# Attention shares of a graph network read from two PSUM banks in turn by the multiplication with the values

## The reference

```
q, k, v = x@qw+qb, x@kw+kb, x@vw+vb          # (N, 8 heads, 16)
alpha = sum(q[dst] * k[src], -1) * SCALE
a = exp(alpha - segment_max(alpha, dst)[dst])
a = a / segment_sum(a, dst)[dst]
out = segment_sum(v[src] * a[:, :, None], dst).reshape(N, 128) + x@sw + sb
```

## Time and profile before

| what | value |
|---|---|
| median of 3 runs | 7398.97 us (7388.78 to 7423.69) |
| the profiled execution | 7369.88 us, span 7368.1 us |
| edge stages of the two convolutions | about 160 to 1565 us and 1700 to 3075 us of the span |
| busy over the span | PE 47%, DVE 55%, ACT 21%, POOL 57% |
| granted TensorE clock over the span | 0.64 |

### The profile page before, as it was taken

How to read it: one execution, slowest core, us unless ns; L and a number is a source line. 1 busy time by engine, 2 the same in 40 slices (tenths; PEclk the granted TensorE clock), 3 DMA queues, 4 the chain that set the end, 5 groups by cost and what they waited for, 6 DMA issues and landing times. The chain is left out here.

```text
span 7368.1 us, 52378 instructions
## 1 busy us (share of the span) xinstructions
PE 3449.0 (47%) x13922; PEld 2171.5 (29%) x13922; DVE 4050.4 (55%) x5309; ACT 1566.7 (21%) x3305; POOL 4165.2 (57%) x4238
## 2 busy tenths in 40 slices
PE   4556565664566565684233334323333422333456
PEld 3445444453455444542011111111111101111223
DVE  5556666664666666675344444434555344445498
ACT  1111111111111111102222222222222222222223
POOL 2556555635565656435766664766665676667321
PEclk7666666675666666786556656555565655556577
DMA  3455555534555555374223232322322222323242
GB/s 100 133 154 159 149 156 155 158 96 138 152 166 152 160 154 157 93 276 109 86 88 93 93 95 70 97 81 91 97 94 88 81 87 83 93 92 98 98 152 89
DMA packets 542429, 877.90 MB, mean 119 GB/s; under 512 B 85288, under 2 KB 383761, under 8 KB 534092
## 3 DMA queue, kind: packets, MB, share of 16 engines
q0 software_dynamic: 167776, 479.21, 21.8%
q1 hardware_dynamic: 374376, 395.35, 17.1%
HBM read 553.75 MB, written 320.47 MB: 119 GB/s over the span
## 5 line engine op out<-in xcount | busy, mean ns | idle before, releaser
L1330 POOL DMA_INDIRECT big<-h_tab,big x2352 | 2245.3, 955 | 1147.8 <-issue 824.1
L598 POOL DMA_INDIRECT big<-kv_tab,big x1664 | 1625.5, 977 | 1185.6 <-DVE big L808 663.4
L1376 PE MATMUL psum<-big 128*128 128x512 f32 x1176 | 1057.8, 1052 | 2255.7 <-ACT big L1353 1292.5
L1413 DVE TENSOR_TENSOR psum<-psum,big 128x1024 f32<-128x1024 f32 x294 | 556.1, 1892 | 1761.4 <-remote 1278.6
L1376 PEld LDWEIGHTS psum<-big 128*128 128x128 f32 x1176 | 333.0, 313 | 2818.8 <-ACT big L1353 1427.8
L1347 ACT COPY big<-big 128x1024 f32<-128x1024 f32 x294 | 567.4, 1930 | 2514.8 <-DVE big L1396 2030.9
L725 PE MATMUL psum<-big 128*128 128x128 bf16 x1408 | 568.7, 404 | 952.4 <-ACT big L679 479.1
L769 PE MATMUL psum<-big 128*128 128x136 f32 x3328 | 777.4, 392 | 184.9 <-DVE big L839 81.4
L679 ACT COPY big<-psum 125x128 f32<-125x128 f32 x1408 | 376.5, 267 | 2042.6 <-PE psum L725 818.0
L769 PEld LDWEIGHTS psum<-big 128*128 128x128 f32 x3328 | 668.7, 281 | 247.1 <-issue 205.3
L803 DVE TENSOR_TENSOR big<-psum,big 128x512 f32<-128x512 f32 x416 | 286.7, 689 | 804.1 <-remote 632.7
(11 more groups left out here) (392 smaller groups left out, 3376.1 us busy)
## 6 DMA issues: line engine op xcount, KB each, us to landing
run_tab<-big SPq DMA_DIRECT2D x294, 512.0 KB
snap_tab<-big SPq DMA_DIRECT2D x176, 448.0 KB
item_tab<-big SPq DMA_DIRECT2D x208, 272.0 KB
big<-loc_tab SPq DMA_DIRECT2D x104, 512.0 KB
big<-h_tab,big POOLq DMA_INDIRECT x2352
big<-kv_tab,big POOLq DMA_INDIRECT x1664
snap_tab<-big SPq DMA_DIRECT2D x176, 52.0 KB
kv_tab<-big SPq DMA_DIRECT2D x12, 512.0 KB, 2.6
```

The lines of the kernel that those rows point to most:

```text
L598: nc.gpsimd.indirect_dma_start(out=kv_ring[:, b % SLOTS, k, :], out_offset=None, in_=kv_tab, in_offset=bass.IndirectOffsetOnAxis(ap=src_it ...
L1330: nc.gpsimd.indirect_dma_start(out=got[j % RING][:, k * D:(k + 1) * D], out_offset=None, in_=h_tab, in_offset=bass.IndirectOffsetOnAxis(ap ...
L1376: ins_ = nc.tensor.matmul(bank[2 * (j % DEEP) + k][:, :], ea_T[j % DEEP], w_blocks[:, k * 512:(k + 1) * 512], start=True, stop=True)
L1413: nc.vector.tensor_tensor(by_feature(msg[j % DEEP]), by_feature(msg[j % DEEP]), got[j % RING].rearrange("p (t f) -> p f t", f=D), ALU.add) ...
```

## The change

The transposes of the exponentials go alternately to bank 3 (even groups) and bank 6 (odd groups), and write their columns already in the order item, half, head: runs of 8 columns with a step of 16. ACT's copy into `share` stays, now without reordering, and L700 still reads `share`. The multiplication with the values reads the shares from the PSUM bank; it waits for `shared` as before. PE waits for the copy of the group before last in place of the last one, and in addition for `va_done` of the group before last, whose shares lay in the bank that it overwrites. No instruction changes its place.

```diff
+                turned_ex = [bank[3], bank[6]]
@@ ACT
                                 act.wait_ge(ex_T, g + 1)
                                 later(act, va_done, 8 * (g - 1))
-                                nc.scalar.copy(by_item(share[g % 2]), bank[3][:, 0:PAIR].rearrange("p (s i h) -> p s i h", s=2, h=HEADS)).then_inc(shared, 1)
+                                nc.scalar.copy(share[g % 2], turned_ex[g % 2][:, 0:PAIR]).then_inc(shared, 1)
@@ PE
                                 pe.wait_ge(ex_done, g + 1)
-                                later(pe, shared, g)
+                                later(pe, shared, g - 1)
+                                later(pe, va_done, 8 * (g - 1))
                                 for s in range(2):
-                                    ins_ = nc.tensor.transpose(bank[3][:, s * P:(s + 1) * P], ex[:, s * P:(s + 1) * P], ident[:, :])
+                                    ins_ = nc.tensor.transpose(by_item(turned_ex[g % 2][:, 0:PAIR])[:, s, :, :], ex[:, s * P:(s + 1) * P], ident[:, :])
                                 ins_.then_inc(ex_T, 1)
@@ DVE
                                 dve.wait_ge(shared, b // 8 + 1)
                                 later(dve, item_done, 2 * b - 2)
                                 nc.vector.tensor_tensor(va[b % 2][:, :, 0:D]..., kv[:, b % SLOTS, :, D:]...,
-                                                        share[b // 8 % 2][:, b % 8 * 32:(b % 8 + 1) * 32]....to_broadcast([P, 4, HEADS, CH]),
+                                                        turned_ex[b // 8 % 2][:, b % 8 * 32:(b % 8 + 1) * 32]....to_broadcast([P, 4, HEADS, CH]),
                                                         ALU.mult).then_inc(va_done, 1)
```

More of the change, by code:

```diff
@@ L808, in _ @@
                                 nc.vector.tensor_tensor(va[b % 2][:, :, 0:D].rearrange("p k (h c) -> p k h c", h=HEADS), kv[:, b % SLOTS, :, D:].rearrange("p k (h c) -> p k h c", h=HEADS),
-                                                        share[b // 8 % 2][:, b % 8 * 32:(b % 8 + 1) * 32].rearrange("p (k h) -> p k h", h=HEADS).unsqueeze(3).to_broadcast([P, 4, HEADS, CH]),
+                                                        turned_ex[b // 8 % 2][:, b % 8 * 32:(b % 8 + 1) * 32].rearrange("p (k h) -> p k h", h=HEADS).unsqueeze(3).to_broadcast([P, 4, HEADS, CH]),
                                                         ALU.mult).then_inc(va_done, 1)
```

## The result

The kernel with the change took 7440.25 us (median, 7420.12 to 7450.84) against 7396.96 us (7380.41 to 7423.69) for the kernel before on the same chip: 1.0054 [1.0038, 1.0070]. That is +43 us, where -4 was forecast, and it lies above the range. The profiled execution took 7450.84 us (span 7449.1), 81 us more than that of before. The execution of before lies 11 us under the fastest of the six timed ones (7380.41), and that of after is the slowest of its six, so this pair overstates the loss: the traces tell where it lies, and the medians how much it is.

What follows compares the result with a forecast made beforehand. No engine was full; POOL's gathers and DVE wait for each other in a ring with four batches between. DVE's +2.5 and POOL's -6.3 us gave about -4, other terms 0: 7399 to 7395 us, range 7356 to 7434.

Steps and rivals of the forecast that it cites:

- The waits: PE's looser wait for ACT's copy and its added wait at L741: all costed at 0.
- ACT's copy and the transposes: L687 without reordering, 394 ns against 387, and PE's stepped PSUM writes at 421 ns: both costed at 0.
- my straight line: ACT's dense copy of 256 columns, interpolated between 298 ns for 128 and 587 for 512: 394 ns.
- the bound of +20 us: Upper bound for PE's transposes, if stepped PSUM writes doubled their duration: at most about 20 us of the end.
- The multiplication, DVE's part: L808 with its second input in PSUM: 6 ns more for each of 416 instances, as L803, +2.5 us.
- Rivals B and C: L808 slower: B by PSUM reads of a repeated element, about 7475, chance 0.07; C by the skill's fixed term, 7440, 0.03.
- The multiplication, POOL's part: Gathers starting in L808 no longer stretched: POOL spared 12.7 us, half reaching the end, -6.3 us (bounds -12.7 and 0).
- The sum: Whole kernel: about -4 us, 7395 us; shifted meetings with other transfers taken as scatter of about 20 us either way.
- rival D: Edge stages: earlier gathers land ahead of other transfers and save long DVE waits, 42 us faster, about 7355, chance 0.10.
- The idle sums: POOL's idle time at L598 (663 us) and DVE's at L803 (633) should each stay within some 30 us.
- the 37: Refutation test: the forecast is wrong if the two edge stages together move by more than 37 us from 2780.

Runs made afterwards that it cites:

- few gathers: Three of four gathers left out from the 15th batch on: kernel before 0.8703 (6438.15 us), changed kernel 0.8695 (6432.38 us).
- The odd and even batches: Changed kernel with the shares read from SBUF again in even batches only, 1.0014, or in odd batches only, 1.0054, of the kernel before.
- five further comparisons: Without, with the change: rerun 1, 1.0038; slots back later 1.0092, 1.0106; fifteen slots 1.0008, 1.0039; one-hot ahead 0.9916, 0.9984; POOL memset 1.0013, 1.0108.
- a later release: POOL waits for the one-hot instead of the multiplication before reusing a slot: kernel before 1.0092, changed kernel 1.0106.
- the plain pair: The kernel before and the changed kernel with no other edit: 1.0054, and 1.0038 when run again.
- the one-hot first: DVE's one-hot moved ahead of the reduction, right behind the multiplication: kernel before 0.9916 (7284.7 us), changed kernel 0.9984 (7328.99 us).
- the memset in the changed kernel: Changed kernel with a one-column memset on POOL ahead of each batch's gathers: 1.0108 of the kernel before.

## Why the prediction was wrong

- **The waits: right as far as shown.** All of the change but the read is 0.9999, the added wait alone 1.0000. With the read there, the kernel that keeps the old wait too is at 1.0023, so that the looser wait has no share in the loss is not shown.
- **ACT's copy and the transposes: right.** No gain depends on the copy; it takes 374 ns instead of 387, better than the 394 of my straight line. PE writes runs of 8 with a step of 16 at 421 ns; the bound of +20 us was not needed.
- **The multiplication, DVE's part: right in substance, off in sign.** I put it at +6 ns, by L803; it is -6 ns (677 against 683), so -2.5 us rather than +2.5. With few gathers the changed kernel is no slower (6 us faster, within the intervals). Rivals B and C needed 89 and 65 ns more per instance: they fell.
- **The multiplication, POOL's part: the step that failed.** Its local half held: of 94 gathers that start in L810, none is stretched. I then took each one's excess as saved for POOL ("POOL is spared 12.7 us") and bounded what it is worth by -12.7 and 0. The first is false as the trace after has it: the next gather comes 0.2 us earlier and starts early enough in L818, 66 of 81 times with a hold-up, and the mean is 976 ns, not 969. The second is where the sign went wrong. I let a gather that isn't held up be at worst useless ("else they are lost in POOL's next wait"). The odd and even batches show that the read which removes these hold-ups in even turns costs 0.54%, and the one that keeps them there 0.14% or nothing.
- **The sum.** "An engine that shifts by a fraction of a microsecond also meets other transfers [...] I can't size that and treat it as scatter." It was no scatter but +43 us, and slower again in four of five further comparisons. The prediction's rival D had this mechanism but with a gain; its own words, that a shifted order "is as likely to be worse", should have been a second rival with a chance of its own.
- **The idle sums.** I wanted L598 and L803 to stay within 30 us. L803's counterpart has 6 us more in all, L598's wait for slots 75 more (663 to 738). The stages moved by 73 us in the traces, and the medians by 43, both beyond the 37 that I named as the refutation.

The Trainium skill, SBUF — State Buffer, section "Who interferes with whom", says that a VectorE instruction with two SBUF inputs contends with a GpSimd instruction that reads SBUF. The counts agree (96 of 99 against 0 of 94, and 257 of 271 in the one-hot); what it is worth to the kernel's time does not follow from it.

What stays open: how 0.13 us at a gather tips a turn of 6.7 us. I have the switch (the read in even turns) and its outcome, not the chain between them, nor why the loss is not seen with a later release, and may be smaller with the old wait. The pattern of waits goes with the loss in the plain pair, but not in the pair with the one-hot first, which still shows the gap.

## What to carry to other kernels

Where no engine is full and two of them wait for each other by turns, contention that is removed is not time gained: ask what starts earlier and what it then meets, count where it lies (here by the instruction under each gather's start), and give a loss its own chance. Here edits that shift the ring by tenths of a microsecond moved the time between 0.84% down (the one-hot first) and 1.08% up (the memset in the changed kernel), and some did nothing; a forecast for such an edit should carry at least half a per cent either way. Test it by applying the edit to half of the turns: equal counts at other places tell a price per instruction from an effect of timing.

## What the runs showed of the hardware

**A PSUM input is not dearer.** DVE with 512 elements takes 689 ns with its first input in PSUM, 677 with its second there, even for a share that is read 16 times in a row, and 683 with both in SBUF. A transpose that writes PSUM in runs of 8 with a step of 16 takes as long as a dense one.

**Products reach a waiting engine late around POOL's gathers.** At the start of the stage POOL issues without a pause until 215 us. In the code, the copies of ACT (L680) shown here wait for nothing but PE's product L726. PE's timeline after, ACT's and POOL's:

```profile
179.68 0.40 PE L726 MATMUL psum<-big 128*128 128x128 bf16 x1 [5.18 <-ACT big L680]
190.24 0.40 PE L726 MATMUL psum<-big 128*128 128x128 bf16 x1 [9.52 <-issue]
...
212.67 0.40 PE L726 MATMUL psum<-big 128*128 128x128 bf16 x1 [2.42 <-issue]
...
221.78 0.40 PE L726 MATMUL psum<-big 128*128 128x128 bf16 x1 [8.07 <-ACT big L680]
```

```profile
189.83 0.27 ACT L680 COPY big<-psum 125x128 f32<-125x128 f32 x1 [10.29 <-remote]
208.76 0.27 ACT L680 COPY big<-psum 125x128 f32<-125x128 f32 x1 [18.66 <-remote]
...
221.37 0.27 ACT L680 COPY big<-psum 125x128 f32<-125x128 f32 x1 [8.84 <-remote]
222.22 0.27 ACT L680 COPY big<-psum 125x128 f32<-125x128 f32 x1 [0.58 <-PE psum L726]
```

```profile
214.05 0.95 POOL L598 DMA_INDIRECT big<-kv_tab,big  x1 [0.30 <-issue]
249.17 0.94 POOL L598 DMA_INDIRECT big<-kv_tab,big  x1 [34.17 <-DVE big L810]
```

The copy starts 9.75 and 18.1 us behind the product's end in the first two cases. The copy at 221.37 is still 8.3 us behind its product, though POOL's last gather ended at 215.0; from 222.22 on it is 0.04 us. So the delay outlasts POOL's issuing by some us, and transfers on their way are as good a candidate as the issuing. Over the whole kernel the copy starts more than 1 us behind its product 401 times of 1408 before, and 76 times with three quarters of the gathers left out (ACT's other waits are in both counts). Whether PE's end, its signal or something else is late, the trace does not say (ends on PE are modelled). It may be why a run of gathers that goes undisturbed is no gain; that link was not tested.
